# A gated cross-attention and expert block on one core: the softmax sums come from the maxima scores on ScalarE, with six head slots and a new order of the work

## What is computed

```
q = layernorm(x) @ Wq.T + bq ;  k = ctx @ Wk.T + bk ;  v = ctx @ Wv.T + bv      # 8 x 512 x 512, 16 heads of 32
attn = softmax(q k^T / sqrt(32))                                                # over the 512 keys
x1 = x + tanh(g_xattn) * ((attn v) @ Wo.T + bo)
probs = softmax(layernorm(x1) @ router_w + router_b)                            # 8 experts
out = x1 + tanh(g_ffn) * max(probs) * (layernorm(x1) @ expert_w[argmax] + expert_b[argmax])
```

## Time and profile before

| what | value |
|---|---|
| time of the runs | 1144.06, 1148.18, 1184.27 us (median 1148.18) |
| profiled execution, span of core 0 | 1149.5 us |
| granted TensorE clock, mean | 0.966 of full speed |
| PE busy | 1021.9 us (89%) |
| DVE busy | 804.2 us (70%) |
| POOL busy | 671.0 us (58%) |
| ACT busy | 513.6 us (45%) |

### The profile page before, as it was taken

One profiled execution on the slowest core, in us unless ns is written; L12 is line 12 of the kernel. 1 busy time (PEld: TensorE's weight loads), 2 busy tenths in 40 slices (PEclk: granted clock), 3 DMA queues, 4 the chain that ended last, 5 costly groups with the idle time before them and its releaser, 6 DMA issues. The chain is left out here.

```text
span 1149.5 us, 19046 instructions
## 1 busy us (share of the span) xinstructions
PE 1021.9 (89%) x5464; PEld 650.7 (57%) x5464; DVE 804.2 (70%) x1748; ACT 513.6 (45%) x920; POOL 671.0 (58%) x446
## 2 busy tenths in 40 slices
PE   3788899989998999899999999999899765889985
PEld 2554566546754674476457655755565323666764
DVE  5655756877696669767975896688667758687554
ACT  4244643563456345534544454445443425333431
POOL 3046655774487448745873686557545646555553
PEclk9898999999999999999999999999999967899998
DMA  7324232523252334333423442243223722444431
GB/s 233 76 75 119 69 80 70 141 77 98 66 140 78 89 84 129 75 84 85 138 66 84 108 124 79 72 119 102 77 64 88 234 102 83 156 130 147 137 123 54
DMA packets 70884, 119.39 MB, mean 104 GB/s; under 512 B 17854, under 2 KB 18878, under 8 KB 70656
## 3 DMA queue, kind: packets, MB, share of 16 engines
q1 hardware_dynamic: 62496, 98.96, 31.4%
q0 software_dynamic: 6240, 18.68, 5.3%
q10 hardware_dynamic: 2048, 0.53, 0.2%
HBM read 50.42 MB, written 18.66 MB: 60 GB/s over the span
## 5 line engine op out<-in xcount | busy, mean ns | idle before, releaser
L691 ACT ACTIVATE probs<-sc 128x512 f32<-128x512 f32 x512 | 279.3, 598 | 205.2 <-PE sc L499 163.1
L1101 POOL TENSOR_TENSOR psum_keys<-psum_keys,probs 128x1024 f32<-128x1024 f32 x128 | 303.8, 2387 | 109.8 <-ACT probs L691 109.6
L826 DVE TENSOR_REDUCE maxima<-jb 128x1 f32<-128x512 f32 x512 | 322.5, 680 | 61.2 <-PE jb L519 60.4
L1101 POOL TENSOR_TENSOR psum_keys<-probs 128x1024 f32<-128x1024 f32 x64 | 153.5, 2413 | 231.2 <-ACT probs L691 231.2
L519 PE MATMUL jb<-k_stack,q_stack 96*128 96x512 f32 x512 | 192.9, 430 | 25.1 <-issue 9.1
L499 PE MATMUL sc<-q_stack,k_stack 98*128 98x512 f32 x512 | 193.1, 427 | 10.1 <-DMA q_stack<-max_rows 8.3
L509 PE MATMUL hb<-probs,values 128*32 128x512 f32 x1024 | 140.4, 626 | 16.4 <-DVE heads_raw L845 7.9
L519 PEld LDWEIGHTS jb<-k_stack,q_stack 96*128 96x128 f32 x512 | 95.5, 193 | 101.2 <-issue 40.3
L499 PEld LDWEIGHTS sc<-q_stack,k_stack 98*128 98x128 f32 x512 | 95.1, 193 | 83.5 <-ACT probs L691 29.9
L861 DVE SCALAR_TENSOR_TENSOR k_lo<-jb,bias,k_hi 128x512 fp32r<-128x512 f32 x32 | 23.9, 747 | 64.0 <-ACT k_hi L710 64.0
L667 PE MATMUL sc<-e_hi,heads_hi 128*128 x156 | 67.4, 432 | 1.0 <-issue 0.5
(11 more groups left out here) (230 smaller groups left out, 1883.0 us busy)
## 6 DMA issues: line engine op xcount, KB each, us to landing
k_stack<-k_hi SPq DMA_DIRECT2D x256, 64.0 KB, 2.0
q_stack<-q_hi SPq DMA_DIRECT2D x256, 64.0 KB, 2.0
stage<-in_x SPq DMA_DIRECT2D x63, 256.0 KB, 3.0
stage<-in_ctx_t SPq DMA_DIRECT2D x32, 256.0 KB, 3.0
k_stack<-k_lo SPq DMA_DIRECT2D x128, 64.0 KB, 2.0
q_stack<-q_lo SPq DMA_DIRECT2D x128, 64.0 KB, 2.0
e_lo<-in_ew SPq DMA_DIRECT2D x8, 1024.0 KB, 12.3
rows<-row SPq DMA_DIRECT2D x30, 257.5 KB
```

The costliest lines, as they stand in the source:

```text
L691: nc.scalar.activation(probs[:, kt % 2, h, :], scs[(16 * g + n) % NSC][:], ACT.Exp, scale=SCALE)\
L826: nc.vector.tensor_reduce(maxima[g % 2][:, n:n + 1], jbs[j][:], AX.X, ALU.max).then_inc(s["mx_done"], 1)
L1101: nc.gpsimd.tensor_tensor(psum_keys[:, two, :], in0, probs[:, kt % 2, two, :], ALU.add)\
```

## The change

- A and SUM are gone, and with them the reciprocal, the two transposes and the multiplication on VectorE. `psum_keys`, `heads_raw` and `sums` are no longer used (late buffers of the same sizes take their places at the end).
- In their place a new ScalarE step ME0 to ME15 (L707 of the kernel after) runs exp over each M bank, in place, with the negated row maximum as bias, and its accumulator output gives the row's sum. An M bank is free only after it. One LN (L711) takes the logarithm of a group's 16 sums, and LT on VectorE subtracts it from the negated maxima. MT, MD and S then bring (-maximum - logarithm) into the score product, so that E gives probabilities that are already normalized.
- The scale 1/sqrt(32) is put into the query weights and bias at the start. `maxima` holds negated maxima, and the rows of `k_stack` hold +1.
- NM reads `hb` itself (ScalarE with the bias, then NL); P0 of the next group waits for NL. heads_hi and heads_lo have six slots instead of four.
- C and NX are wholly on GpSimd: it makes the rounded copy (L1079) and the difference, and applies scale and shift to x (L1091).
- The two DMAs of MD go from ScalarE's queue to SP's. SQ and SK are split by head in SP's table.
- All order tables are new, and a table of digits, BANK_TABLE, names the `jb` bank of each user. The scratch for dynamic DMAs is set to 8192. Tables for Exp and Ln are loaded once, as one set.

```
-THROUGH_JB = {"M", "MT", "V", "SUM", "Q", ...
+THROUGH_JB = {"M", "MT", "V", "Q", ...
...
+NHEADS = 6
...
-                found[item] = turn % NJB
+                found[item] = int(digits[turn]) if turn < len(digits) else turn % NJB
...
+                elif kind == "MD":
+                        sp.dma_start(q_stack[g % 2][MAXROW + k:MAXROW + k + 1, :].bitcast(F32),
+                                     max_rows[HD * k:HD * k + 16, :].bitcast(F32)).then_inc(s["max_rows_in"], 16)
...
-                        wait(pe, s["nm_chain"], g)
+                        wait(pe, s["nm_done"], g)
...
-                    jb_held(j, s["mx_done"], 16 * g + n + 1)
+                    jb_held(j, s["me_done"], 16 * g + n + 1)
                 elif kind == "MT":
-                    pe.wait_ge(s["mx_done"], 16 * (g + 1))
+                    pe.wait_ge(s["lt_done"], g + 1)
...
-                elif kind == "SUM":
-                    pe.wait_ge(s["acc_done"], 6 * (g + 1))
...
-                    wait(act, s["acc_done"], 6 * g + (h2 + 1 if kt >= 2 else 2 * kt - 4 + h2 + 1))
-                    nc.scalar.activation(probs[:, kt % 2, h, :], scs[(16 * g + n) % NSC][:], ACT.Exp, scale=SCALE)
+                    nc.scalar.activation(probs[:, kt % 2, h, :], scs[(16 * g + n) % NSC][:], ACT.Exp)
...
-                    act.wait_ge(s["nm_chain"], g + 1)
+                    act.wait_ge(s["pv_done"], NT * (g + 1))
...
+                elif kind == "ME":
+                    act.wait_ge(s["mx_done"], 16 * g + n + 1)
+                    nc.scalar.activation(jbs[j][:], jbs[j][:], ACT.Exp, bias=maxima[g % 2][:, n:n + 1],
+                                         accum_out=row_sums[g % 2][:, n:n + 1]).then_inc(s["me_done"], 1)
+                elif kind == "LN":
+                    act.wait_ge(s["me_done"], 16 * (g + 1))
+                    nc.scalar.activation(row_sums[g % 2][:], row_sums[g % 2][:], ACT.Ln).then_inc(s["ln_done"], 1)
...
+                elif kind == "LT":
+                    dve.wait_ge(s["ln_done"], g + 1)
+                    nc.vector.tensor_tensor(maxima[g % 2][:], maxima[g % 2][:], row_sums[g % 2][:], ALU.subtract)
...
-                elif kind == "A":
-                    nc.gpsimd.tensor_tensor(psum_keys[:, two, :], in0, probs[:, kt % 2, two, :], ALU.add)
...
 LAST, SP:
-        "~~RW2 ~~RW3 1SQ 1SK ^DC0 ^DC1 2SQ ^DC2 ^DC3 ~DR2 2SK ~RW0 ~DR3 ^DX0 ^DX1 ~RW1 ^DX2 3SQ 3SK ^0SQ ^DX3 ^0SK DR0",
+        "3SQ0 3SQ1 3SQ2 2MD 3SK1 ~RW1 ~RW0 3SQ3 3SK2 3SK3 3MD",
```

More of the change, by code:

```diff
@@ L204, in banks @@
     found = {}
-    for b, table in bodies():
+    for (b, table), digits in zip(bodies(), BANK_TABLE):
         turn = 0
         for (_, _, kind, _), item in zip(tokens_of(table, "PE"), items_of(table, "PE", b)):
-            if kind in THROUGH_JB:
-                found[item] = turn % NJB
+            if kind in THROUGH_JB and item is not None:
+                found[item] = int(digits[turn]) if turn < len(digits) else turn % NJB
                 turn += 1
@@ L307, in build @@
         max_rows = sb("max_rows", [P, P], F32R)
+        row_sums = [sb(f"row_sums{i}", [P, 16]) for i in range(2)]
         st1 = [rt[:, 48 + 12 * i:60 + 12 * i] for i in range(2)]
@@ L527, in item @@
                     jb_held(j, s["mt_lo"], g + 1)
-                elif kind == "SUM":
-                    pe.wait_ge(s["acc_done"], 6 * (g + 1))
-                    jb_free(j)
-                    for h in range(HG):
-                        last = nc.tensor.matmul(jbs[j][h * HD:(h + 1) * HD, :], ones[:], psum_keys[:, h, :],
-                                                start=True, stop=True)
-                    last.then_inc(s["sum_mm"], 1)
-                    jb_held(j, s["wide_done"], g + 1)
                 elif what == "Q":
@@ L580, in item @@
                     wait(pe, s["w_lo_done"], 3 * NF + k + 1)
[L581 removed]
+                    at = (NG * t + k) % NHEADS
+                    last = three(jbs[j][:], heads_hi[:, at, n * P:(n + 1) * P], heads_lo[:, at, n * P:(n + 1) * P],
                                  w_hi[3][:, k, :], w_lo[3][:, k, :], k)
```

185 lines of the change are left out of this document (78 added, 107 removed), and 131 rows, old and new, of tables (CLOSING, LAST, OPENING, ORDER).

## The result

| | before | after |
|---|---|---|
| runs | 1144.06 to 1184.27 us (4), median 1147.84 | 1053.13 to 1061.78 us (4), median 1057.68 |
| ratio after / before | | 0.9204, 95% interval 0.9161 to 0.9247 |
| profiled execution | span 1149.5 | span 1056.0, time 1057.68 |

The ratio is taken over runs in the faster of the chip's two states, without the run of 1184.27 us; it differs a little from the ratio of the two medians.

What follows compares the result with a forecast made beforehand. TensorE's work and how promptly VectorE, ScalarE and GpSimd empty the banks were taken to set the pace. 1149.5 - 28 (SUM) - 10 (old waits) + 10 (new waits) + 2 (start) - 18 (end) = 1105.5, left at 1105 us; range 1072 to 1150.

Steps and rivals of the forecast that it cites:

- SUM goes: 28 us: TensorE: removing 31 SUM blocks at 0.9 us each saves 28 us, bounds 27 and 34.
- -10 for the waits that go: TensorE: idle time ahead of SUM goes, 12.7 us less 3 at the end, so 10 us saved.
- +10 for new waits, the cover is the new order: M and S matmuls wait longer behind ScalarE's MEs: 10 us added, the new order covering the rest.
- The other bound of 29 us for the waits: Waits ahead of SUM counted by its weight loads: 31.8 us less 3 at the end.
- Rival 1: ScalarE becomes the bound: accumulator output costs a second instruction, ME 0.95 us, 1185 us in all; chance 0.11.
- A separate accumulator row: ScalarE's trace: a row of its own for ME's accumulator, or ME above 0.9 us, would show the forecast wrong.
- rival 4: ScalarE: Exp and Ln change tables, two loads a group of 1.283 us, +82 us, 1187 us; chance 0.01.
- Rival 3: MD in SP's queue behind 24 stack DMAs: each S0 could come 1 us later, +32 us, 1137; chance 0.04.
- Rivals 2 and 5: 2: longer chains eat TensorE's gain, 1135 us, chance 0.18. 5: larger savings on SUM, waits and end, 1076 us, 0.14.
- Start +2: Start: GpSimd's longer chain before the first Q, ME and LN before the first transpose: +2 us (-4 to +6).
- The end: End of attention: heads_hi follows the last P sooner, the P0 wait goes, clock gains: 18 us saved, bounds 5 and 24.

Runs made afterwards that it cites:

- e12: SUM's four matmuls put back on constant data, nothing waiting for them, against e1: 1137.46 us, ratio 0.9869 to the kernel before.
- e1: Kernel before with the row sums left out (no A, SUM, SC; NM multiplies by a constant), old order: 1138.77 us, ratio 0.9899.
- e16: SUM's matmuls put on constant data into the first seven batches of the changed kernel, nobody waiting for them: 1093.8 us, ratio 0.9523 to before.
- e15: Operations of e1 (no sums) in the changed kernel's order, bank table, six head slots and SP table: 1061.18 us, ratio 0.9235 to before.
- e3: Changed kernel with ME, LN and LT left out, so no row sums, in the new order: 1042.79 us, ratio 0.9081 to before.
- e6: Changed kernel with ME's accumulator output removed, LN reading a constant: 1049.69 us, ratio 0.9141 to before.
- e7: Changed kernel with MD back in ScalarE's queue behind MT: 1076.99 us, ratio 0.9369 to before.
- e13: e1 with MD and the stack loads by head in SP's queue, by the changed kernel's SP table: 1162.61 us, ratio 1.0091 to before.
- e18: The changed kernel run once more, unedited, on another chip: 1072.78 us, ratio 0.9245 to before.
- e9: e1 with NM by ScalarE from hb, six head slots, C and NX on GpSimd, old order: 1162.51 us, ratio 1.0006 to before.

## Why the prediction was right and wrong

**What bounds the kernel.** Right in naming TensorE and the emptying of the banks; wrong in treating TensorE's work as a price that is paid one for one in any order. "SUM goes: 28 us" fails there. In the order of before this work cost nothing (e12 against e1), and when it went, idle time and the lower clock took its place. In the new order 25 us of it cost some 36, part of them waits for a bank (e16). The term has no value without the order that it stands in.

**The waits.** The main failed step is here. "-10 for the waits that go" and "+10 for new waits, the cover is the new order" is where the 39 us of the middle are missing: 27.2 us a group were forecast, 25.93 measured. I priced the new order only as a cover for what it adds, at no gain of its own. e1 against e15 puts that gain at 69 us of the middle: 30 less idle, 39 less busy time for the same matmuls, most of it the clock. No term of the sum had the clock in the middle, since the earlier trace rows show 1.00 from 213 to 745 us; the 20.5 us at the lower level lay between the first and the last transpose but outside that stretch. The other bound of 29 us for the waits was nearer than the one taken, but for another reason than given: SUM's waits gone are worth nothing in e1.

**ScalarE.** Right. ME was taken at 0.65 us and is 0.66 in a run; 23.0 us a group were forecast, 22.6 measured. Rival 1 had the mechanism (a second instruction of 0.22 us is there) but not the price. A separate accumulator row was even named as a sign of being wrong; it came, and cost 0.09 us an ME. The two table loads are there as forecast, and rival 4 is out. The waits of M and S for their banks are 95.7 us against 64.8, up by 31 where 10 was forecast. Before, 34.9 of them were on VectorE, so those on ScalarE alone rose by 66. They cost little: without ME (e3) the middle is only 18 us shorter.

The Trainium skill, on the page ScalarE: Activation LUTs, section What ACT_TABLE_LOAD costs, gave an estimate of 614 ns for such an activation in a row. e6 shows 567 to 600, so the estimate is high by 2 to 8%. The Trainium skill, on the page VectorE: DVE Perf Modes, section Two Vector instructions with no wait between them, counts an accumulating operation as two instructions, for VectorE. ScalarE's trace agrees with the count and not with a full second start: 0.09 us, not 0.26.

**GpSimd and MD.** Copy and scaling at the lower bounds, hidden as forecast: GpSimd's 5.1 us a group were forecast as 6.3. Rival 3 (MD in SP's queue costs) is out for this order, and its sign was wrong: back on ScalarE it costs 19 us (e7). In the old order SP's new table did cost 2% (e13), so this price too depends on the order.

**Rivals 2 and 5.** The chains that eat the gain (1135) did not come. The better case (1076), held at 0.14, was nearest and still 18 us short, and by other terms than those that gave the gain: it took SUM at 34 us and had nothing for the order. That the forecast had the direction right is therefore partly luck.

**Start and end.** Start +2 forecast, -0.5 measured. The end was forecast at -18 and is -26.3 in the two traces. To the first product 18 were forecast and 12.3 measured: heads_hi came in time, but the first product comes 50.5 us after the last transpose, not 45. The other 14.0 lie in the products, for which the sum has no term. On two chips the new tables alone shorten that stretch by 5 to 9 us. The rest goes with the "remote" waits, 13.0 us of which are in the trace of before and none in that of the changed kernel; e18 has 22.9 and takes 17.5 us longer. So only a part of the 14 us can be given to the change.

**Still open.** Which part of the old order holds the groups at 28 us when nothing needs it any more was not found: not SP's table with MD in it (e13, which left the waits for the landing of the maxima standing), not the places (e9), not SUM's work (e12). The tables of the engines were changed only together, and a rotation of the banks inside the new order was not tried, so what the bank table is worth isn't known.

## What to carry to other kernels

In a hand-ordered pipeline, operations and order are one design: price a removal by the order that it makes possible, and when a change comes with new tables, give the order a term and a range of its own (here 6.6%, against 1% for the removed work). The busiest engine's work can be taken as a price only if idle time doesn't fill the place that it leaves: put dummy work in or take work out, and see whether the group moves. And look whether an edit removed the wait that it was to remove, before its time is read (e13). Compare kernels by their middle stretch and by ratios of one chip; totals of two chips differed by 15 us for the same kernel.

## What the runs showed of the hardware

- An activation that writes a row sum has a record ACTIVATION_READ_ACCUMULATOR of 0.22 us, of which 0.09 us show in the distance of starts (0.660 against 0.567 us at 128 x 512 in PSUM). An exp from PSUM to SBUF without bias starts 0.48 us after the one before.
- Stalls of TensorE can cost twice, as idle time and by the clock: all 11 falls to 1.2 GHz in e1's middle followed a stretch in which TensorE was less busy than its mean. With the same matmuls, e1 and e15 differ by 30 us of idle and 39 us of busy time, and the lower level stood for 64.9 and 10.2 us of their middles.
- GpSimd's copy of 128 x 512 float32 took 0.62 us and its scale and shift by two columns 0.79 us, no more than ScalarE's 0.63 and 0.82. Its own two-input pass of the same size took 1.29 us.
- The expert products, with their gathers and scatters, took 146.7 us on one chip and 164.2 on another, with the attention equal to 0.01 us a group. The second trace has 22.9 us of waits that the profile calls "remote", the first none.
